# Feed-forward stages: transposes and low-rank product issued one schedule step earlier

## The chip, the cores and the metric

The kernel runs on one core of a Trainium2 chip. The metric is the device time of one execution in microseconds. TensorE (PE), VectorE (DVE), ScalarE (ACT), GpSimd (POOL) and SyncE (SP, which issues DMAs) each run their own instruction stream in order, and meet by semaphores.

## The reference

The input `x` is 8 x 1024 tokens of 256 float32 values. Four layers follow, each added to its own input:

```python
x = x + attn_a(layernorm(x))     # recurrent mixer
x = x + ffn(layernorm(x))
x = x + attn_b(layernorm(x))     # softmax attention, 16 heads
x = x + ffn(layernorm(x))        # the same weights

def ffn(x, fast_b, w_fc, w_proj, u, v, gate):
    h = bitlinear(x, w_fc) + gate * (x @ v.T @ fast_b.T @ u.T)   # 256 -> 1024, and rank 16
    r = maximum(h, 0)
    return bitlinear(r * r, w_proj)                              # 1024 -> 256
```

`bitlinear` multiplies by weights that are rounded to -1, 0 or 1, with a scale per output.

## The kernel before

Each of the four layers is a stage of the kernel, one after the other. The change is in `feed_forward`, which runs twice (names with `ffn_` in the profile; the rest, `a_` and `b_`, is not touched).

A feed-forward stage works on 16 chunks of 512 tokens. The work on a chunk has three parts:

- **normalize**: VectorE finds mean and variance (lines 1217, 1221), GpSimd makes the reciprocal root (1294, 1296), VectorE writes the normalized tokens `xn` in four tiles (1233). TensorE transposes them in two groups of four (1043). ScalarE copies a group to `x_hi`, rounded to the matmul's input format (1120), and VectorE writes the rest, `x_lo` (1240). TensorE makes the low-rank product from both in four matmuls (1053), ScalarE and VectorE turn it into `low` (1128, 1247). The moments of the next chunk are taken at the end of the part.
- **up**: eight times, five matmuls of 512 columns, the fifth with `low` (1065, 1066, 1069). ScalarE applies relu (1137) and square (1141), VectorE splits the square into `r_hi` (1261) and `r_lo` (1263).
- **down**: for each of four token tiles, 16 matmuls of 256 columns (1082, 1083). VectorE scales the result (1274) and GpSimd adds it to `x` (1319).

The parts of three chunks run interleaved: `down(c)`, `up(c + 1)` and `normalize(c + 2)` form one turn. Each part is a Python generator with eight steps. `side_by_side` takes one step of each part in rotation, down first, then up, then normalize, and it does so on every engine for itself:

```python
while running:
    part = min(running, key=lambda r: (r[2] + 0.5) / r[0])
    if next(part[1], running) is running:
        running.remove(part)
    part[2] += 1
```

So the place of an instruction in its engine's queue is set by the step in which its generator issues it. A bare `yield`, or `steps(n)`, which is n of them, is an empty step: it moves what follows behind one more piece of down and of up. A piece of down on TensorE is half a token tile (10 matmuls, then 6), a piece of up is one tile of the hidden layer. There are 18 turns in a stage: the first has normalize alone, the second up and normalize, then come 14 full ones, one without normalize, and one with down alone. Two banks of PSUM hold the transposes and the low-rank product by turns.

Of the kernel before, what the change touches and what calls it, by code (L numbers as in the profile page):

```python
# [906 lines left out]
def feed_forward(nc, banks, x_in, x_out, d, tag, prepared):  # L907
    with nc.cleanup_on_exit(), ExitStack() as ctx:
# [64 lines left out]
        def steps(n):  # L973
            for _ in range(n):
                yield

        def schedule(down, up, normalize):
            for c in range(-2, CHUNKS):
                side_by_side(*([(DOWN, down(c), 1)] if c >= 0 else []),
                             *([(UP, up(c + 1), 1)] if 0 <= c + 1 < CHUNKS else []),  # L980
                             *([(NORMALIZE, normalize(c + 2), 1)] if c + 2 < CHUNKS else []))

        def ternary_turns():

            fc_part = [(m, m, 0, KT) for m in range(HT)]
            return fc_part, [(FC_TURNS + m * (HT // CT) + n, m, n * CT, CT) for m in range(KT) for n in range(HT // CT)]

        def tensor(pe):
            def prepare_weights():
                if not first_use:  # L990
                    pe.wait_ge(kept_moved, 16 * len(kept))
                    return

                def turn_ternary(turns, first_row):
                    for turn, m, at, count in turns:
                        b, s = banks[:, turn % 5, :], tern[(first_row + m) % 2]
                        pe.wait_ge(tern_made, first_row + m + 1)
                        if turn >= 5:
                            pe.wait_ge(tern_t_made, turn - 4)
                        for i in range(count):  # L1000
                            last = pe.transpose(b[:, i * P:(i + 1) * P], s[:, (at + i) * P:(at + i + 1) * P], ident[:, :])
                        last.then_inc(tern_turned, 1)

                fc_part, proj_part = ternary_turns()
                pe.wait_ge(x_lo_made, KT)
                turn_ternary(fc_part, 0)
                pe.wait_ge(weights_in, 16 * WEIGHTS)
                pe.wait_ge(u_steps, 5)
                for m in range(HT):
                    if m >= 2:  # L1010
                        pe.wait_ge(u_t_made, m - 1)
                    pe.transpose(banks[0:ROWS, 5 + m % 2, 0:P], u3[:, m, :], ident[:, :]).then_inc(u_turned, 1)
                for kt in range(KT):
                    if kt:
                        pe.wait_ge(low_copied, 1)
                    pe.matmul(banks[:, 7, 0:RANK], v[:, kt * P:(kt + 1) * P], fast_b[:, :],
                              start=True, stop=True).then_inc(low_product, 1)
                turn_ternary(proj_part, HT)
                for kt in range(KT):
                    pe.wait_ge(diagonal_made, kt + 1)  # L1020
                    if kt:
                        pe.wait_ge(row_made, 1)
                    pe.matmul(banks[:, 7, 0:P], ones[:, :], diagonal[:, kt, :], start=True, stop=True).then_inc(row_ready, 1)
                pe.wait_ge(tern_t_made, FC_TURNS + PROJ_TURNS)
                pe.wait_ge(row_made, KT)
                pe.wait_ge(low_split, 2)
                pe.wait_ge(u_t_made, HT)

            def normalize(c):
                x_hi, x_lo = x_hi_bufs[c % 2], x_lo_bufs[c % 2]  # L1030
                yield from steps(3)
                for kt in range(KT):
                    b = normal[(3 * c + kt) % 2]

                    chunk, part = divmod(3 * c + kt - 2, 3)
                    if chunk >= 0 and part == 2:
                        pe.wait_ge(low_made, chunk + 1)
                    elif chunk >= 0:
                        pe.wait_ge(x_lo_made, 2 * chunk + part + 1)
                    for i in range(CT):  # L1040
                        if kt == 0:
                            pe.wait_ge(xn_made, CT * c + i + 1)
                        last = pe.transpose(b[:, i * P:(i + 1) * P], xn[i][:, kt * P:(kt + 1) * P], ident[:, :])  # L1043
                    last.then_inc(xn_turned, 1)
                    yield
                if c == 0:
                    prepare_weights()
                yield
                b = normal[(3 * c + 2) % 2]
                pe.wait_ge(x_lo_made, 2 * c + 2)  # L1050
                passes = [(kt, w, s) for kt in range(KT) for w, s in ((low_by_hi, x_hi), (low_by_lo, x_lo))]
                for n, (kt, w, s) in enumerate(passes):
                    last = pe.matmul(b[0:ROWS, :], w[:, kt, :], s[:, kt, :], start=n == 0, stop=n == len(passes) - 1)  # L1053
                last.then_inc(low_ready, 1)
                yield from steps(2)

            def up(c):
                x_hi, x_lo, low = x_hi_bufs[c % 2], x_lo_bufs[c % 2], low_bufs[c % 2]
                for m in range(HT):
                    use, cols = HT * c + m, slice(m * P, (m + 1) * P)  # L1060
                    b = high[use % 3]
                    if use >= 3:
                        pe.wait_ge(relu_made, use - 2)
                    for kt in range(KT):
                        pe.matmul(b, fc_t[:, kt, cols], x_hi[:, kt, :], start=kt == 0, stop=False)  # L1065
                        pe.matmul(b, fc_t[:, kt, cols], x_lo[:, kt, :], start=False, stop=False)  # L1066
                    if m == 0:
                        pe.wait_ge(low_made, c + 1)
                    pe.matmul(b, u3_t[:, cols], low[:, :], start=False, stop=True).then_inc(h_ready, 1)  # L1069
                    yield  # L1070

            def down(c):
                par = c % 2
                for i in range(CT):
                    use = CT * c + i
                    b = back[use % 3]
                    if use >= 3:
                        pe.wait_ge(y_scaled, use - 2)
                    for m in range(HT):
                        if i == 0:  # L1080
                            pe.wait_ge(r_lo_made, HT * c + m + 1)
                        pe.matmul(b[:, 0:DIM], r_hi[par][:, m, i * P:(i + 1) * P], proj_t[:, m, :], start=m == 0, stop=False)  # L1082
                        last = pe.matmul(b[:, 0:DIM], r_lo[par][:, m, i * P:(i + 1) * P], proj_t[:, m, :],  # L1083
                                         start=False, stop=m == HT - 1)
                        if m == HT // 2:
                            yield
                    last.then_inc(y_ready, 1)
                    yield

            pe.wait_ge(ident_in, 16)  # L1090
            schedule(down, up, normalize)

        def scalar(act):
# [18 lines left out]

            def normalize(c):
                x_hi, low = x_hi_bufs[c % 2], low_bufs[c % 2]
                yield from steps(3)
                for kt in range(KT):
                    act.wait_ge(xn_turned, 2 * c + kt + 1)
                    if c >= 2:
                        act.wait_ge(h_ready, HT * (c - 1))
                    act.activation(x_hi[:, kt, :], normal[(3 * c + kt) % 2], ACT.Copy).then_inc(x_hi_made, 1)  # L1120
                    yield
                if c == 0:
                    prepare_weights()
                yield
                act.wait_ge(low_ready, c + 1)
                if c >= 2:
                    act.wait_ge(h_ready, HT * (c - 1))
                act.activation(low[:, :], normal[(3 * c + 2) % 2][0:ROWS, :], ACT.Copy).then_inc(low_hi_made, 1)
                yield from steps(2)

            def up(c):
                for m in range(HT):
# [11 lines left out]
            def down(c):  # L1144
                for _ in range(DOWN):
                    yield

            schedule(down, up, normalize)

        def vector(dve):  # L1150
# [73 lines left out]
            def normalize(c):  # L1224
# [7 lines left out]
                for i in range(CT):  # L1232
                    dve.tensor_scalar(xn[i][:, :], x[:, i, :], mean_var[:, i, 0:1], norm_rstd[:, i:i + 1],
                                      ALU.subtract, ALU.mult).then_inc(xn_made, 1)
                yield from steps(2)
                for kt in range(KT):
                    dve.wait_ge(x_hi_made, 2 * c + kt + 1)
                    if c >= 2:
# [4 lines left out]
                if c == 0:  # L1243
# [2 lines left out]
                dve.wait_ge(low_hi_made, c + 1)  # L1246
                dve.tensor_tensor(low[SUB:2 * SUB, :], normal[(3 * c + 2) % 2][SUB:2 * SUB, :],
                                  low[SUB:2 * SUB, :].bitcast(F32), ALU.subtract).then_inc(low_made, 1)
                yield
                if c + 1 < CHUNKS:  # L1250
                    take_moments(c + 1)
                yield
# [904 lines left out]
```

## Time and profile before

| | us |
|---|---|
| median of 3 runs | 3332.47 |
| lowest, highest | 3331.1, 3334.16 |
| profiled execution | 3332.47 |
| its span in the profile | 3330.7 |

The two feed-forward stages take about 375 and 335 us of the span. In the profile an engine is busy while it works on an instruction; matmul ends are modelled, so the start of the next matmul is the better mark. Idle time stands with the event that ended it. A share of busy time says little by itself here; what counts is which wait on TensorE ends last.

### The profile page before, as it was taken

What the parts mean: (1) busy time and instruction counts of PE and PEld (TensorE: products, weight loads), DVE (VectorE), ACT (ScalarE), POOL (GpSimd) and SP (SyncE); (2) the same over time, 40 slices, a digit from 0 to 9 for tenths busy, and PEclk for the clock granted to TensorE, in tenths of its full rate; (3) what the DMA queues carried; (4) which work ended last, traced back from release to release, by engine and by line L of the source; (5) the groups of instructions that cost most, each with busy time, mean ns of one, the idle gap of its engine ahead of it and who ended that gap; (6) DMA issues with size and microseconds to landing.
All of it is one profiled execution on the core that took longest, in us unless ns stands there. A gap on an engine that the chain in (4) does not pass through costs nothing. (4 is left out here: it accounts for less than half of the span.)

```text
span 3330.7 us, 78935 instructions
## 1 busy us (share of the span) xinstructions
PE 3141.0 (94%) x31780; PEld 1962.2 (59%) x31780; DVE 2521.4 (76%) x4844; ACT 1984.0 (60%) x2967; POOL 784.5 (24%) x920
## 2 busy tenths in 40 slices
PE   7999999995999589999999999999999999987999
PEld 3666666663888445555555555555555555546888
DVE  6877777755888368878878788788787887827887
ACT  2545555533666217676767676667676767775665
POOL 3444455432223201011021020110210201011222
PEclk8999999986999759999999999999999999998999
DMA  1000000003111512122222131222221312103111
GB/s 53 15 21 21 27 27 27 21 16 103 51 51 52 108 29 46 25 46 50 46 50 46 25 70 25 46 50 46 50 45 25 70 26 45 37 4 102 51 58 39
DMA packets 110301, 145.50 MB, mean 44 GB/s; under 512 B 21745, under 2 KB 94209, under 8 KB 109153
## 3 DMA queue, kind: packets, MB, share of 16 engines
q1 hardware_dynamic: 108728, 136.78, 17.6%
q8 instruction: 252, 4.13, 0.5%
q0 software_dynamic: 768, 2.77, 0.4%
q10 hardware_dynamic: 440, 0.90, 0.2%
q14 instruction: 113, 0.92, 0.1%
HBM read 53.79 MB, written 38.24 MB: 28 GB/s over the span
## 5 line engine op out<-in xcount | busy, mean ns | idle before, releaser
L1883 DVE TENSOR_REDUCE b_half_max<-banks 128x1 f32<-128x512 f32 x2048 | 1305.0, 685 | 300.9 <-PE banks L1556 184.4
L1807 ACT ACTIVATE b_p_t<-banks 128x1024 f32<-128x1024 f32 x1024 | 1039.6, 1026 | 372.7 <-PE banks L1556 231.6
L1632 PE MATMUL banks<-b_k_stack,b_q_stack 62*128 62x512 f32 x2048 | 836.1, 481 | 35.3 <-issue 19.4
L1694 PE MATMUL banks<-b_q_stack,b_k_stack 64*128 64x512 f32 x2048 | 832.5, 469 | 8.5 <-ACT b_p_t L1807 7.7
L1648 PE MATMUL banks<-b_p_t,b_v 128*17 128x256 f32 x8192 | 628.4, 385 | 0.2 <-ACT b_p_t L1807 0.2
L1694 PEld LDWEIGHTS banks<-b_q_stack,b_k_stack 64*128 64x128 f32 x2048 | 344.5, 185 | 372.8 <-issue 323.2
L1632 PEld LDWEIGHTS banks<-b_k_stack,b_q_stack 62*128 62x128 f32 x2048 | 342.0, 188 | 85.2 <-DVE b_half_max L1883 34.0
L1556 PE MATMUL banks<-b_unit,b_tables 64*128 64x64 bf16 x4096 | 373.3, 197 | 0.0
L1137 ACT ACTIVATE ffn_relu<-banks,ffn_scale_fc 128x512 f32<-128x512 f32 x256 | 176.1, 688 | 206.0 <-PE banks L1069 206.0
L1082 PE MATMUL banks<-ffn_proj_t,ffn_r_hi 128*128 128x256 f32 x1024 | 262.2, 289 | 2.7 <-DVE ffn_r_lo L1263 2.5
L1556 PEld LDWEIGHTS banks<-b_unit,b_tables 64*128 64x128 bf16 x4096 | 186.3, 96 | 120.9 <-issue 72.2
L1083 PE MATMUL banks<-ffn_proj_t,ffn_r_lo 128*128 128x256 f32 x1024 | 253.8, 280 | 0.0
L1648 PEld LDWEIGHTS banks<-b_p_t,b_v 128*17 128x17 f32 x8192 | 142.4, 95 | 168.6 <-ACT b_p_t L1807 59.2
L1972 POOL TENSOR_TENSOR b_qk_lo<-b_qk,b_qk_hi 128x512 fp32r<-128x512 f32 x64 | 81.8, 1279 | 607.7 <-ACT b_qk L1749 461.5
L1082 PEld LDWEIGHTS banks<-ffn_proj_t,ffn_r_hi 128*128 128x128 f32 x1024 | 193.5, 189 | 18.0 <-DVE ffn_r_lo L1263 8.6
L1065 PE MATMUL banks<-ffn_x_hi,ffn_fc_t 128*128 128x512 f32 x512 | 203.3, 397 | 0.0
L1066 PE MATMUL banks<-ffn_x_lo,ffn_fc_t 128*128 128x512 f32 x512 | 202.9, 396 | 0.0
L1083 PEld LDWEIGHTS banks<-ffn_proj_t,ffn_r_lo 128*128 128x128 f32 x1024 | 193.3, 189 | 8.2
L1263 DVE TENSOR_TENSOR ffn_r_lo<-ffn_square,ffn_r_hi 128x512 fp32r<-128x512 f32 x256 | 188.9, 738 | 8.8
L1319 POOL TENSOR_TENSOR ffn_x<-ffn_x,ffn_scaled_out 128x256 f32<-128x256 f32 x128 | 112.9, 882 | 339.8 <-DVE ffn_scaled_out L1274 339.8
L1261 DVE CAST ffn_r_hi<-ffn_square 128x512 fp32r<-128x512 f32 x256 | 127.3, 497 | 74.8 <-ACT ffn_square L1141 73.2
L1141 ACT ACTIVATE ffn_square<-ffn_relu 128x512 f32<-128x512 f32 x256 | 161.9, 632 | 8.1
(246 smaller groups left out, 4941.1 us busy)
## 6 DMA issues: line engine op xcount, KB each, us to landing
ffn_x<-x SPq DMA_DIRECT2D x32, 512.0 KB, 3.9
b_q_stack<-b_qk_hi SPq DMA_DIRECT2D x252, 64.0 KB
b_k_stack<-b_qk_hi SPq DMA_DIRECT2D x252, 64.0 KB
a_x<-hidden_states SPq DMA_DIRECT2D x16, 512.0 KB, 4.2
x<-a_x SPq DMA_DIRECT2D x16, 512.0 KB, 2.9
x<-ffn_x SPq DMA_DIRECT2D x16, 512.0 KB, 2.8
b_x<-x SPq DMA_DIRECT2D x8, 1024.0 KB, 5.7
x<-b_x SPq DMA_DIRECT2D x8, 1024.0 KB, 4.4
```

Of the source, the lines that this page charges most:

```text
L1065: pe.matmul(b, fc_t[:, kt, cols], x_hi[:, kt, :], start=kt == 0, stop=False)
L1066: pe.matmul(b, fc_t[:, kt, cols], x_lo[:, kt, :], start=False, stop=False)
L1082: pe.matmul(b[:, 0:DIM], r_hi[par][:, m, i * P:(i + 1) * P], proj_t[:, m, :], start=m == 0, stop=False)
L1083: last = pe.matmul(b[:, 0:DIM], r_lo[par][:, m, i * P:(i + 1) * P], proj_t[:, m, :], start=False, stop=m == HT - 1)
L1137: act.activation(relu[use % 2][:, :], high[use % 3], ACT.Relu, scale=scale_fc[:, m:m + 1]).then_inc(relu_made, 1)
L1263: dve.tensor_tensor(r_lo[par][:, m, :], square[use % 2][:, :], r_hi[par][:, m, :].bitcast(F32), ALU.subtract).then_inc(r_lo_made, 1)
L1556: last = pe.matmul(out[:, cols], tables[rows, g % GROUPS * PAIRS + pair, 1 - variant, part, :], unit[rows, :], start=False, stop=part == P ...
L1632: last = pe.matmul(m, q_stack[rows, slot, qb * P:(qb + 1) * P], k_stack[rows, slot, half * BANK:(half + 1) * BANK], start=True, stop=not h ...
L1648: last = pe.matmul(values[i * SLOT:i * SLOT + VW, cols], v[:, kb, hg * GROUP + i, :], p_t[(2 * t + i % 2) % P_BUFS][:, i // 2, cols], star ...
L1694: last = pe.matmul(out, k_stack[stack, slot, kb * P:(kb + 1) * P], q_stack[stack, slot, half * BANK:(half + 1) * BANK], start=True, stop=n ...
L1807: act.activation(p_t[use % P_BUFS][:, :, :], scores[use % 2], ACT.Exp, scale=slopes()[pair][0]).then_inc(p_made, 1)
L1883: dve.tensor_reduce(half_max[:, (pair + rg * PAIRS) * QB + qb, half:half + 1], misc.at["max", g, turn], axis=AX.X, op=ALU.max, negate=True ...
```

## The change

Three parts of `normalize` change, one for each of TensorE, ScalarE and VectorE. On all three the empty steps ahead of the first transposes, or of what uses them, are one fewer, and those at the end of the part one more. On VectorE the tiles `xn` stay in the second step and the moments in the eighth. GpSimd's `normalize` is not touched, nor are down, up and SyncE.

```diff
@@ tensor, normalize(c)
-                yield from steps(3)
+                yield from steps(2)
                 for kt in range(KT):
                     b = normal[(3 * c + kt) % 2]
...
                 last.then_inc(low_ready, 1)
-                yield from steps(2)
+                yield from steps(3)
@@ scalar, normalize(c)
-                yield from steps(3)
+                yield from steps(2)
                 for kt in range(KT):
                     act.wait_ge(xn_turned, 2 * c + kt + 1)
...
                 act.activation(low[:, :], normal[(3 * c + 2) % 2][0:ROWS, :], ACT.Copy).then_inc(low_hi_made, 1)
-                yield from steps(2)
+                yield from steps(3)
@@ vector, normalize(c)
                     dve.tensor_scalar(xn[i][:, :], x[:, i, :], mean_var[:, i, 0:1], norm_rstd[:, i:i + 1],
                                       ALU.subtract, ALU.mult).then_inc(xn_made, 1)
-                yield from steps(2)
+                yield
                 for kt in range(KT):
                     dve.wait_ge(x_hi_made, 2 * c + kt + 1)
...
                                   low[SUB:2 * SUB, :].bitcast(F32), ALU.subtract).then_inc(low_made, 1)
-                yield
+                yield from steps(2)
                 if c + 1 < CHUNKS:
                     take_moments(c + 1)
```

The first group of transposes goes from the fourth step to the third, the second from the fifth to the fourth, the low-rank product from the seventh to the sixth, and what ScalarE and VectorE make of each goes with it.

## Rows read from the trace of the kernel before

**Rows 1.** The page, part 1: busy us, share, instructions.
```profile
PE 3141.0 (94%) x31780; PEld 1962.2 (59%) x31780; DVE 2521.4 (76%) x4844; ACT 1984.0 (60%) x2967; POOL 784.5 (24%) x920
```
**Rows 2.** Busy us by stretch, one turn each (PE PEld DVE ACT POOL, clock, DMA).
```profile
879.00:898.00 19.00, 19.00 (x118) 16.61 (x117) 16.48 (x36) 12.03 (x19) 5.34 (x6) 1.00 0.17 56
3182.50:3201.49 18.99, 18.98 (x118) 16.51 (x116) 16.47 (x36) 12.02 (x19) 5.36 (x6) 1.00 0.18 56
```
**Rows 3.** The chain that ended last, second stage: start, us, what.
```profile
3042.13 0.47 PE banks L1043 x4
...
3288.95 0.47 PE banks L1043 x4
3291.77 0.44 PE banks L1043 x4
...
3296.43 0.92 PE banks L1053 x4
```
**Rows 4.** Waits over the whole span: us in total, times, longest.
```profile
PE banks L1043 <- DVE ffn_xn L1233: 32.8, 4, 18.1
PEld banks L1082 <- DVE ffn_r_lo L1263: 8.6, 30, 1.5
```
**Rows 5.** Timeline of one turn, TensorE: start, us, what.
```profile
3184.91 0.40 PE L1069 MATMUL banks<-ffn_low,ffn_u_t 80*128 80x512 f32 x1
...
3187.84 0.28 PE L1083 MATMUL banks<-ffn_proj_t,ffn_r_lo 128*128 128x256 f32 x1
3188.14 0.39 PE L1082 MATMUL banks<-ffn_proj_t,ffn_r_hi 128*128 128x256 f32 x1
...
3189.41 0.39 PE L1069 MATMUL banks<-ffn_low,ffn_u_t 80*128 80x512 f32 x1
...
3191.97 0.29 PE L1082 MATMUL banks<-ffn_proj_t,ffn_r_hi 128*128 128x256 f32 x1
...
3193.86 0.64 PE L1043 MATMUL banks<-ffn_ident,ffn_xn 128*128 128x128 f32 x4
3194.24 0.37 PE L1082 MATMUL banks<-ffn_proj_t,ffn_r_hi 128*128 128x256 f32 x1
```
**Rows 6.** Timeline of the same turn, VectorE (idle time and releaser in brackets).
```profile
3184.39 0.69 DVE L1263 TENSOR_TENSOR ffn_r_lo<-ffn_square,ffn_r_hi 128x512 fp32r<-128x512 f32 x1
...
3185.82 0.42 DVE L1274 TENSOR_TENSOR ffn_scaled_out<-banks,ffn_scale_row 128x256 f32<-128x256 f32 x1
3186.73 0.62 DVE L1261 CAST ffn_r_hi<-ffn_square 128x512 fp32r<-128x512 f32 x1 [0.48 <-ACT ffn_square L1141]
...
3191.23 0.43 DVE L1261 CAST ffn_r_hi<-ffn_square 128x512 fp32r<-128x512 f32 x1
...
3192.30 1.81 DVE L1233 TENSOR_SCALAR ffn_xn<-ffn_x,ffn_mean_var,ffn_norm_rstd 128x256 f32<-128x256 f32 x4
...
3200.58 0.87 DVE L1261 CAST ffn_r_hi<-ffn_square 128x512 fp32r<-128x512 f32 x1 [0.24 <-ACT ffn_square L1141]
```
**Rows 7.** Timeline of the same turn, GpSimd.
```profile
3186.33 0.74 POOL L1319 TENSOR_TENSOR ffn_x<-ffn_x,ffn_scaled_out 128x256 f32<-128x256 f32 x1 [4.16 <-DVE ffn_scaled_out L1274]
...
3200.42 0.74 POOL L1319 TENSOR_TENSOR ffn_x<-ffn_x,ffn_scaled_out 128x256 f32<-128x256 f32 x1 [3.96 <-DVE ffn_scaled_out L1274]
```
**Rows 8.** Timeline of the second stage's second turn, TensorE.
```profile
3024.34 0.39 PE L1066 MATMUL banks<-ffn_x_lo,ffn_fc_t 128*128 128x512 f32 x1
3024.57 0.40 PE L1069 MATMUL banks<-ffn_low,ffn_u_t 80*128 80x512 f32 x1
3025.68 1.21 PE L1043 MATMUL banks<-ffn_ident,ffn_xn 128*128 128x128 f32 x4 [0.71 <-DVE ffn_xn L1233]
...
3031.30 0.46 PE L1053 MATMUL banks<-ffn_x_hi,ffn_low_by_hi 128*80 128x512 f32 x1 [0.45 <-DVE ffn_x_lo L1240]
```
**Rows 9.** TensorE alone by stretch: busy us (instructions), clock, DMA share, GB/s.
```profile
2978.00:2984.00 6.00, 3.57 (x35) 1.00 0.00 0
...
2996.00:3002.00 6.00, 0.00 (x0) 0.50 0.52 175
```

## The prediction

> **What bounds the kernel now.** I read the page first: TensorE is busy for 94% of the span [rows 1]. The change touches only the two feed-forward stages, so their stretches come next. One turn of the schedule has the same busy times in both: TensorE has work in all 19 us at a granted clock of 1.00, VectorE in 16.5, ScalarE in 12.0 [rows 2]. The chain that ended last shows how regular that is. The first transposes of a turn stand at 3042.13 us, those 13 turns later at 3288.95, so a turn lasts 18.99 us [rows 3]. A turn costs what TensorE's queue takes, waits included, and the reader must see which waits are in it. The list of waits gives two. The transposes waited for `xn` four times in the whole run, too few for the 28 full turns. The down product's weight load waited for `r_lo` 30 times, 8.6 us together [rows 4].
>
> **How near the edge that is.** The timelines of one turn, engine by engine, say when each thing is ready. I write Dk, Uk, Nk for the k-th piece of down, up and normalize, T0 and T1 for the two groups of transposes, L for the low-rank products. TensorE's order is D1 U1 N1 D2 U2 N2 and so on. Before, T0 stands in N4, T1 in N5, L in N7, and VectorE writes `xn` in N2.
> - U2's closing matmul starts at 3189.41 [rows 5]. Its result goes through ScalarE to VectorE, whose r_hi starts at 3191.23; r_lo and then the four `xn` follow, 3192.30 to 3194.11 [rows 6].
> - TensorE does D3 and U3 until 3191.97, D4 and U4 until 3193.86, and then T0; D5 begins at 3194.24 [rows 5]. The fourth transpose needs the fourth `xn`, which ended at 3194.11, and D5 begins 0.13 us after that. In the chain T0 takes 0.47 us and T1, whose inputs have long been there, 0.44 [rows 3]. So T0 arrives within some hundredths of the moment from which it would have to wait. There is no slack to spend.
>
> **The change part by part.** No instruction is added or removed: three counts of empty steps change on TensorE, ScalarE and VectorE. `xn` stays in VectorE's N2 and the moments in its N8; T0, T1, L and the conversions behind them go one step forward. GpSimd and SyncE keep their order, and no DMA moves.
>
> *T0 from N4 to N3.* TensorE now reaches T0 at 3191.97 in the picture of that turn, but the fourth `xn` still ends at 3194.11, because what leads to it (U2, ScalarE, r_hi, r_lo, four `xn`) is not moved. TensorE resumes at 3194.24, the same time as before, but with D4 and U4 still to do. Their length is 3191.97 to 3193.86, 1.89 us, and nothing later gives it back, as all that follows is TensorE's own work. Behind the waiting transposes the queue holds D4, U4 and the rest of the turn; ScalarE and VectorE wait for those in turn, and have time to spare. Cost: 1.89 us a turn.
>
> *T1 and L.* T1 follows U4; its inputs are there and its bank is free. In the chain L stands 4.66 us behind T1 (3291.77 to 3296.43), two pieces of down and two of up apart [rows 3], and it will again. Counted from D4's start, L is reached at 1.89 and 4.66, 6.55 us. It needs the second half of x_lo. U4's closing matmul starts at about 1.65, r_hi comes 1.82 us behind a closing matmul (3186.73 after 3184.91), the pair r_hi and r_lo takes 1.15 and x_lo about 0.7 as r_lo does: 5.3 us. So it is covered, by 1.2 us, and beyond that L would wait for the difference. U1 of the next turn, which uses the low result, has it a step sooner than before. Cost: nothing.
>
> *L out of the gap between U7 and U8.* L took 0.92 us [rows 3] between U7 and D8. With it gone, all that hangs on U7 comes 0.92 us later as seen from U8. VectorE's r_lo of U7 ends at 3186.00 in place of 3185.08; the low result, which followed it, is away, so the scaled output starts at 3186.03 [rows 6]. GpSimd's addition starts 0.51 us behind it (3186.33 after 3185.82) and takes 0.74: 3186.54 to 3187.28 [rows 6, 7]. r_hi of U8 starts at 3186.73, inside it. Where they overlap, r_hi ends 0.28 or 0.29 us after the addition does: 3187.35 after 3187.07, and 3201.45 after 3201.16, where it took 0.87 us and not some 0.43 [rows 6, 7]. So r_hi ends at 3187.56. Before it ended at 3187.35: 0.21 us later.
> The Trainium skill (SBUF — State Buffer, section "SBUF: two separate sides") says that VectorE in its fast modes and GpSimd share a pair of ports, and that whoever starts first locks it for the whole instruction. Those rows agree with it. By it the 0.21 us stands as long as GpSimd starts first, which it does here by 0.19 us, and turns into a gain if r_hi comes first.
>
> *The wait for r_lo in D2.* The last pair of D2 needs r_lo of U8. It starts at 3188.14, 0.30 us after the matmul at 3187.84 [rows 5]. 512 columns take 0.23 us [rows 8], so these 256 would take 0.12, and 0.18 us is wait. It stands ahead of U2 in the queue, so the 0.21 us adds to the turn; the `xn` are late by no more than that. 1.89 and 0.21 are 2.10 us a turn. If r_hi of U8 is free of the addition, it takes 0.19 less and the wait goes: 1.89 less 0.18, 1.71 us.
>
> *The second turn of a stage*, the first with up, has no down part. T0 waited there too: U4's closing matmul starts at 3024.57, T0's four run from 3025.68 and wait for the `xn` [rows 8]. Now U4 (five matmuls, 1.17 us) comes after T0. L waited for x_lo at its end (3031.30, 0.45 us idle before it) [rows 8]. It starts at about the same time in its new place, with U7 still to do. Cost: one U, some 1.1 us, in each stage. The last two turns have no normalize and stay as they are. The very first turn holds normalize alone, and its order does not change.
>
> **The sum.** 28 turns of 2.10 us are 58.8, two such second turns 2.2, together 61.0 us. The profiled execution took 3332.47 us, its span 3330.7, and the median of the runs is also 3332.47: 3393.5 us. The bounds: 1.71 us a turn gives 50.1 and 3382.6 us. For the upper one I take one more meeting of VectorE and GpSimd on the chain in each turn, at the 0.43 us that the full one costs r_hi: 2.53 us a turn, 73.0 and 3405.5 us.
>
> **Rivals.**
> 1. *The collision goes away*, as r_hi of U8 begins ahead of the addition. The stall at T0 stays. For it: only 0.19 us separates the two starts. Against: both hang on the same TensorE order by fixed distances. 3382.6 us.
> 2. *The move is hidden*, so not slower. VectorE has 2.5 us without work in a turn [rows 2], and its four `xn` would come 1.9 us sooner if that slack lay ahead of them. This decides from an `xn` end of 3192.2 in the picture of that turn. With the r_lo wait gone as well (28 times 0.18) it gives 3327.4, without it 3332.5 us. Against: U2's own result reaches r_hi at 3191.23 whatever VectorE does before it, and with the pair and four `xn` behind it the end cannot come much before 3194.
> 3. *The clock falls in the pause.* TensorE would stand for some 2 us in each turn. With no work at all from 2996 to 3002 us the granted clock is 0.50, half of 2.4 GHz; with 3.57 us of work in the 6 us from 2978 it stays at 1.00 [rows 9]. If 6 us of each turn ran at half rate, 3 us more would go in each: 28 times 3.0 is 84, 3477 us.
> The Trainium skill (TensorE: Matmul & The Clock Gate, Part 1) says that the gate closes behind idleness and opens with sustained work. By it this rival is real only if such a pause counts as idle; the row at 2978 speaks against it.
>
> **Chances.** The forecast 0.80, the first rival 0.09, the second 0.06, the third 0.05. About 0.2% (6.7 us) is what can be told from no change here. The second rival lies within it, but for 0.01 in which it goes beyond, to faster. So faster 0.01, same 0.05, slower 0.94. The range goes from just below the first rival to the upper bound, 3380 to 3406 us. It leaves out rivals two and three and a little of the forecast's own error.
>
> **What the profile of the changed kernel would show.** A turn of 21.1 us in both stages in place of 18.99. Waits at the transposes for `xn` in all 30 turns, about 1.9 us each, on TensorE's matmul or its weight load. A wait at the down product for r_lo of 0.4 us, with r_hi of U8 at about 0.83 us. No wait of L for x_lo in the full turns. The clock at 1.00 through the turns. A turn of 20.7 us with r_hi of U8 at 0.43 would show the first rival, one of 19.0 the second, matmuls at half rate behind the pause the third. The forecast is wrong if the first `xn` starts earlier than 2.9 us after U2's closing matmul.

## The result and the profile after

The changed kernel takes 3392.99 us (median of 4, 3391.84 to 3396.83), the kernel before 3333.31 us on the same occasions: a ratio of 1.0168, 95% interval 1.0145 to 1.0192. It is 1.7% slower, and the forecast was 3393.5 us. The profiled execution has a span of 3394.8 us, 64.1 us more than before.

The chain that ended last in the second stage, for [rows 3] (start, us, what). T0 of one turn and of the next:

```profile
3201.92 0.83 DVE ffn_xn L1233
...
3202.89 1.21 PE banks L1043 x4
...
3210.63 0.92 PE banks L1053 x4
...
3223.93 1.21 PE banks L1043 x4
...
3350.27 1.21 PE banks L1043 x4
```

T0 comes every 21.05 us (from 3202.89 to 3350.27 are 7 turns) in place of 18.99. In the chain it is 1.21 us long and was 0.47, and the first `xn` is now a link ahead of it.

The stretches of one turn and of 13 turns, for [rows 2] (length, busy us of PE, PEld, DVE, ACT, POOL, then the granted clock, DMA share and GB/s):

```profile
3202.89:3223.93 21.04, 19.71 (x116) 16.52 (x117) 16.21 (x36) 12.12 (x20) 5.17 (x6) 1.00 0.15 46
```

```profile
3076.59:3350.27 273.68, 256.21 (x1509) 214.79 (x1509) 211.00 (x456) 157.67 (x248) 67.28 (x78) 1.00 0.14 47
```

The work is the same, TensorE has 1.3 us of each turn without any, and the clock stays at its upper level through all 13 turns. The list of waits, for [rows 4] (us in total, times, longest):

```profile
PE banks L1043 <- DVE ffn_xn L1233: 66.0, 32, 18.5
PEld banks L1082 <- DVE ffn_r_lo L1263: 14.9, 30, 1.5
PEld banks L1043 <- DVE ffn_xn L1233: 11.0, 60, 0.2
PE banks L1082 <- DVE ffn_r_lo L1263: 8.8, 30, 1.3
```

The wait for `xn` is now in the 28 full turns too. It has grown by 33.2 us; 2.3 of them lie in the two second turns, and the rest is 1.10 us in each full turn. That is less than the loss. The timeline of TensorE shows why, for [rows 5]:

```profile
3220.09 0.39 PE L1069 MATMUL banks<-ffn_low,ffn_u_t 80*128 80x512 f32 x1
...
3222.43 0.40 PE L1069 MATMUL banks<-ffn_low,ffn_u_t 80*128 80x512 f32 x1
3223.93 1.21 PE L1043 MATMUL banks<-ffn_ident,ffn_xn 128*128 128x128 f32 x4 [1.10 <-DVE ffn_xn L1233]
3224.90 0.37 PE L1082 MATMUL banks<-ffn_proj_t,ffn_r_hi 128*128 128x256 f32 x1
...
3231.52 0.39 PE L1053 MATMUL banks<-ffn_x_hi,ffn_low_by_hi 128*80 128x512 f32 x1
...
3239.36 0.28 PE L1083 MATMUL banks<-ffn_proj_t,ffn_r_lo 128*128 128x256 f32 x1
3239.88 0.38 PE L1082 MATMUL banks<-ffn_proj_t,ffn_r_hi 128*128 128x256 f32 x1 [0.24 <-DVE ffn_r_lo L1263]
```

U3's closing matmul starts at 3222.43 and would be followed 0.23 us later. D4 begins at 3224.90, so T0 takes 2.24 us of the queue, and took 0.38. The loss is 1.86 us. The profile writes only 1.10 of it down as idle, the rest lies mostly between the four transposes, each of which waits for its own `xn`: they are stretched over 1.21 us. VectorE and GpSimd in the same turns, for [rows 6, 7]:

```profile
3222.97 1.78 DVE L1233 TENSOR_SCALAR ffn_xn<-ffn_x,ffn_mean_var,ffn_norm_rstd 128x256 f32<-128x256 f32 x4
...
3229.52 0.68 DVE L1240 TENSOR_TENSOR ffn_x_lo<-banks,ffn_x_hi 128x512 fp32r<-128x512 f32 x1
...
3237.57 0.42 DVE L1274 TENSOR_TENSOR ffn_scaled_out<-banks,ffn_scale_row 128x256 f32<-128x256 f32 x1
3238.25 0.85 DVE L1261 CAST ffn_r_hi<-ffn_square 128x512 fp32r<-128x512 f32 x1 [0.26 <-ACT ffn_square L1141]
```

```profile
3222.40 1.24 POOL L1319 TENSOR_TENSOR ffn_x<-ffn_x,ffn_scaled_out 128x256 f32<-128x256 f32 x1
...
3238.07 0.74 POOL L1319 TENSOR_TENSOR ffn_x<-ffn_x,ffn_scaled_out 128x256 f32<-128x256 f32 x1 [4.55 <-DVE ffn_scaled_out L1274]
```

The fourth `xn` ends at 3224.75, D4 begins 0.15 us later. GpSimd's addition of 3222.40 lies over the first `xn`, which takes 0.83 us in the chain. The addition of 3238.07 starts 0.18 us ahead of r_hi of U8, which takes 0.85 us, and the last pair of D2 starts 0.52 us after the matmul ahead of it, 0.40 more than without a wait. x_lo's second half ends at 3230.20, and L starts at 3231.52, 1.3 us behind it, without a wait.

The second turn of the second stage, for [rows 8]: TensorE was idle for 1.88 us ahead of T0 in place of 0.71, and for 0.47 ahead of L in place of 0.45.

```profile
3059.66 1.21 PE L1043 MATMUL banks<-ffn_ident,ffn_xn 128*128 128x128 f32 x4 [1.88 <-DVE ffn_xn L1233]
...
3065.27 0.46 PE L1053 MATMUL banks<-ffn_x_hi,ffn_low_by_hi 128*80 128x512 f32 x1 [0.47 <-DVE ffn_x_lo L1240]
```

In the second turn of the first stage T0 waits for 1.96 us in place of 0.79, and there the clock falls. The stretches of 3 us, with all engines, then the clock:

```profile
821.00:824.00 3.00, 1.40 (x5) 0.97 (x6) 2.93 (x8) 1.16 (x3) 0.78 (x1) 0.87 1.01 381
824.00:827.00 3.00, 3.00 (x11) 2.36 (x11) 1.18 (x2) 1.43 (x3) 0.00 (x0) 0.56 0.66 209
```

```profile
822.60 1.35 PE L1043 MATMUL banks<-ffn_ident,ffn_xn 128*128 128x128 f32 x4 [1.96 <-DVE ffn_xn L1233]
...
824.61 0.63 PE L1065 MATMUL banks<-ffn_x_hi,ffn_fc_t 128*128 128x512 f32 x1
825.03 0.63 PE L1066 MATMUL banks<-ffn_x_lo,ffn_fc_t 128*128 128x512 f32 x1
```

Matmuls of 512 columns start 0.42 us apart there, and 0.23 us apart in the same place before.

### The profile page after: what moved, and what is told of

Same layout as the page of the kernel before. It is cut to its first block and busy times, and to the rows that moved or that the text cites. A ratio compares the mean times of both kernels' runs of the same rounds, so it can differ in the third digit from the quotient of the medians.

```text
span 3394.8 us, 78935 instructions
## 1 busy us (share of the span) xinstructions
PE 3167.3 (93%) x31780; PEld 1968.3 (58%) x31780; DVE 2514.9 (74%) x4844; ACT 1986.9 (59%) x2967; POOL 779.7 (23%) x920
## 5 line engine op out<-in xcount | busy, mean ns | idle before, releaser
L1082 PEld LDWEIGHTS banks<-ffn_proj_t,ffn_r_hi 128*128 128x128 f32 x1024 | 194.4, 190 | 24.4 <-DVE ffn_r_lo L1263 14.9
L1263 DVE TENSOR_TENSOR ffn_r_lo<-ffn_square,ffn_r_hi 128x512 fp32r<-128x512 f32 x256 | 177.3, 692 | 8.8
```

## The experiments

Two things were to be tested: that the stall at T0 is the distance from U2's result to the fourth `xn` and nothing about the place itself, and that the smaller part is GpSimd's addition meeting r_hi. All kernels compute the whole reference. Turn lengths are distances from one L to the next in full turns. Each ratio is to executions of the kernel before on the same occasions, and not to the 3334.27 in the first row: their median is 3333.31 us for the changed kernel, 3333.78 for the two parts alone, one step more and early moments without the hold, 3334.27 for the rest. One long execution moves a ratio more than it moves a median (the transposes alone have one of 3399.86 us), so the turns tell kernels apart better than the ratios do.

| kernel | turn, us | median, us | ratio to before, 95% interval |
|---|---|---|---|
| before | 18.98 | 3334.27 (23 runs) | |
| changed | 21.05 | 3392.99 (4) | 1.0168, 1.0145 to 1.0192 |
| transposes alone | 20.83 | 3387.29 (4) | 1.0168, 1.0144 to 1.0192 |
| L alone | 20.34 | 3374.21 (4) | 1.0124, 1.0109 to 1.0140 |
| transposes one step more | 24.99 | 3510.29 (4) | 1.0539, 1.0519 to 1.0559 |
| `xn` in N1 | 20.13 | 3369.11 (4) | 1.0101, 1.0088 to 1.0114 |
| `xn` in N1, early moments | 19.18 | 3340.69 (10) | 1.0016, 0.9999 to 1.0033 |
| changed, addition held | 20.65 | 3386.05 (4) | 1.0153, 1.0139 to 1.0166 |
| before, addition held | 18.80 | 3327.36 (12) | 0.9991, 0.9977 to 1.0006 |
| early moments, addition held | 18.78 | 3327.20 (12) | 0.9978, 0.9966 to 0.9990 |

**Transposes alone.** Against the changed kernel, on TensorE (and the same on ScalarE and VectorE):

```diff
                 if c == 0:
                     prepare_weights()
-                yield
+                yield from steps(2)
                 b = normal[(3 * c + 2) % 2]
...
                 last.then_inc(low_ready, 1)
-                yield from steps(3)
+                yield from steps(2)
```

> Only the transposes and x_hi, x_lo go a step forward; the low-rank product L stays in N7. Theory (the fourth xn decides, and L's leaving the gap between U7 and U8 makes the 0.2 us): a turn of 20.88 us (18.99 and 1.89), r_hi of U8 at 0.62 us as before, the wait for r_lo at 0.18 us; 28 times 1.89 and some 1.4 in the second turns, 3387 us. Rival (the later r_lo comes with the transposes, not with L): a turn of 21.06 us and r_hi of U8 at 0.85, 3392 us.

The turn is 20.83 us. VectorE's r_hi of U8:

```profile
3191.65 0.62 DVE L1261 CAST ffn_r_hi<-ffn_square 128x512 fp32r<-128x512 f32 x1 [0.48 <-ACT ffn_square L1141]
```

0.62 us, as before. The list of waits has the load's row for r_lo back at `8.6, 30, 1.5`. The move of the transposes costs 1.85 us a turn and leaves r_hi alone; the other 0.22 us come with L.

**L alone.** Against the kernel before, the `yield` ahead of L goes behind it, on the three engines.

```diff
                 if c == 0:
                     prepare_weights()
-                yield
                 b = normal[(3 * c + 2) % 2]
...
                 last.then_inc(low_ready, 1)
-                yield from steps(2)
+                yield from steps(3)
```

> Only the low-rank product L goes a step forward, to N6; transposes stay in N4 and N5. Theory: in the turn of the trace of before L would be reached at 3198.99, while the second half of x_lo ends at 3200.01, so L waits 1.1 us, and the addition meets r_hi of U8 for 0.21 us more: a turn of 20.3 us, 3371 us. Rival (L costs only the meeting, 0.21 us a turn): 3338 us. No wait at the transposes in either.

```profile
3192.10 0.46 PE L1052 MATMUL banks<-ffn_x_hi,ffn_low_by_hi 128*80 128x512 f32 x1 [0.93 <-DVE ffn_x_lo L1238]
...
3200.51 0.38 PE L1081 MATMUL banks<-ffn_proj_t,ffn_r_hi 128*128 128x256 f32 x1 [0.23 <-DVE ffn_r_lo L1260]
```

On TensorE's timeline L waits for x_lo and D2's last pair for r_lo, as expected; the turn is 20.34 us, 1.36 more than before. So the parts do not add (1.85 and 1.36 alone, 2.07 together): with the transposes a step earlier x_lo comes earlier too, and L's own wait of 1.1 us is covered.

**Transposes one step more.** On TensorE and ScalarE the first group goes to N2, the second to N3; L stays in N6.

```diff
-                yield from steps(2)
+                yield from steps(1)
                 for kt in range(KT):
...
                 if c == 0:
                     prepare_weights()
-                yield
+                yield from steps(2)
```

> Transposes another step forward (first group in N2, second in N3), L in N6. Theory: TensorE reaches the first group 2.33 us (D3 and U3) earlier still, the fourth xn ends at the same distance from U2, so a turn of 23.4 us and some 3459 us, with the granted clock at 1.00. Rival (the clock falls in a pause of 4.2 us a turn): matmuls of 512 columns spaced 0.43 us behind the pause in the turns, 80 us more. Rival (the price is not the distance to xn): no more than the changed kernel, 3393 us.

The theory's time was missed by 51 us. The turn is 24.99 and not 23.4 us. TensorE by stretches of 4 us (length, busy, instructions, granted clock, DMA share, GB/s), and its timeline:

```profile
3200.00:3204.00 4.00, 3.77 (x24) 1.00 0.33 112
3204.00:3208.00 4.00, 0.55 (x4) 0.89 0.44 145
3208.00:3212.00 4.00, 4.00 (x16) 0.50 0.01 5
3212.00:3216.00 4.00, 4.00 (x20) 0.76 0.01 4
3216.00:3220.00 4.00, 4.00 (x27) 1.00 0.00 0
```

```profile
3207.93 1.35 PE L1043 MATMUL banks<-ffn_ident,ffn_xn 128*128 128x128 f32 x4 [3.45 <-DVE ffn_xn L1233]
```

From its list of waits:

```profile
PE banks L1043 <- DVE ffn_xn L1233: 133.3, 32, 18.1
```

The idle time at T0 grew by 67.3 us against the changed kernel; in a full turn it is 3.45 us in place of 1.10, 2.35 more, where 2.33 was expected. The turn grew by 3.94 us. The other 1.6 us go with the clock: by the end of the 3.45 us it has fallen to 0.50, 1.2 GHz, and matmuls run at half rate until it rises. The idle time is the same in every full turn while the turns take 24.4 to 25.8 us, so what varies is not the wait. The rival on the clock, which the full turns of the changed kernel did not show with 1.10 us idle, is real at this length: the kernel takes 51 us more than expected, where the rival had 80.

**`xn` in N1**, in the changed kernel. The wait for `norm_scale` and the four `xn` go ahead of VectorE's first `yield`, and that `yield` behind them.

```diff
                     take_moments(c)
-                yield
                 dve.wait_ge(norm_scale, c + 1)
...
                                       ALU.subtract, ALU.mult).then_inc(xn_made, 1)
-                yield
+                yield from steps(2)
```

> The changed kernel with xn issued in N1 and not N2; moments and reciprocal root stay in the eighth step. Theory (the price of the transposes' place is the time at which the fourth xn ends): xn no longer waits for U2's result but for the reciprocal root, which ends 0.9 us before xn could end now less its own 1.4 us; the fourth xn ends 0.9 us sooner, the turn is 20.2 us, 3368 us. Rival (what is ahead of xn does not matter, the transposes cost by their place): 3393 us.

VectorE's timeline:

```profile
3202.01 1.38 DVE L1232 TENSOR_SCALAR ffn_xn<-ffn_x,ffn_mean_var,ffn_norm_rstd 128x256 f32<-128x256 f32 x4 [0.93 <-POOL ffn_norm_rstd L1295]
```

`xn` now waits for the reciprocal root. The turn is 20.13 us. The transposes stand where they stood, and the loss went from 2.07 to 1.15 us by what ends `xn`. About 0.4 of the gain has a cause that the expectation did not name: the four `xn` take 1.38 us in place of 1.78, as no addition lies over the first of them now.

**`xn` in N1 and early moments.** The same, and the moments of the next chunk in VectorE's fifth step, the reciprocal root in GpSimd's sixth.

```diff
                 if c == 0:
                     prepare_weights()
+                if c + 1 < CHUNKS:
+                    take_moments(c + 1)
                 yield
...
-                yield from steps(2)
-                if c + 1 < CHUNKS:
-                    take_moments(c + 1)
-                yield
+                yield from steps(3)
@@ gpsimd, normalize(c)
-                yield from steps(3)
+                yield
                 if c + 1 < CHUNKS:
                     take_rstd(c + 1)
-                yield
+                yield from steps(3)
```

> The change as it is, with xn moved from VectorE's N2 to N1, and the moments and the reciprocal root that it needs moved from the eighth step to the fifth and sixth. Theory: the fourth xn is there before TensorE reaches the transposes in N3, so that wait goes and only the r_lo wait of 0.39 us stays: a turn of 19.2 us, 3334 to 3338 us. Rival (the earlier place of the transposes costs by something else, a bank or the order itself): the turn stays near 21 us, 3390 us.

From the list of waits, and VectorE's and GpSimd's timelines:

```profile
PE banks L1043 <- DVE ffn_xn L1232: 32.0, 4, 18.1
PEld banks L1082 <- DVE ffn_r_lo L1261: 16.6, 32, 1.5
```

```profile
3208.58 0.43 DVE L1259 CAST ffn_r_hi<-ffn_square 128x512 fp32r<-128x512 f32 x1
3209.05 1.11 DVE L1261 TENSOR_TENSOR ffn_r_lo<-ffn_square,ffn_r_hi 128x512 fp32r<-128x512 f32 x1
```

```profile
3208.66 0.95 POOL L1317 TENSOR_TENSOR ffn_x<-ffn_x,ffn_scaled_out 128x256 f32<-128x256 f32 x1 [1.23 <-DVE ffn_scaled_out L1272]
```

With the transposes in N3 the wait for `xn` is back at four times in the run. The turn is 19.18 us; the median is a little above what was expected. What is left is the r_lo wait, and in a form that the prediction did not have: r_hi starts first and takes 0.43 us, but the addition, which waits for it, then holds up r_lo, 1.11 us in place of 0.69. The trace of the kernel before has the same pattern, in the very turn that the prediction read:

```profile
3195.44 0.43 DVE L1261 CAST ffn_r_hi<-ffn_square 128x512 fp32r<-128x512 f32 x1
3195.90 1.11 DVE L1263 TENSOR_TENSOR ffn_r_lo<-ffn_square,ffn_r_hi 128x512 fp32r<-128x512 f32 x1
```

```profile
3195.58 0.88 POOL L1319 TENSOR_TENSOR ffn_x<-ffn_x,ffn_scaled_out 128x256 f32<-128x256 f32 x1 [2.60 <-DVE ffn_scaled_out L1274]
```

**The held addition**, in three kernels. GpSimd's fourth addition of a chunk waits until r_lo of U8 is made:

```diff
                     pool.wait_ge(y_scaled, use + 1)
+                    if i == CT - 1 and c + 1 < CHUNKS:
+                        pool.wait_ge(r_lo_made, HT * (c + 2))
```

> The changed kernel, with GpSimd's fourth addition of a chunk held until r_lo of U8 is made, so that it can't meet r_hi or r_lo of U8. Theory (the meeting costs 0.4 us on the chain r_hi, r_lo, down product, and the wait for r_lo is nothing but that and 0.0 us): r_hi of U8 0.43 us, no wait for r_lo in D2, a turn of 20.66 us in place of 21.06, 3382 us. Rival (r_hi takes 0.85 us for another reason, or the held addition meets something else on the chain): the turn stays at 21.06, 3393 us. The wait at the transposes stays in both.

> The kernel before, with the same hold on the fourth addition. Theory: r_hi of U8 0.43 in place of 0.62 us, the wait of 0.18 us for r_lo goes, a turn of 18.81 us, 5 us less than before in all. Rival (the held addition delays the moments, the reciprocal root or xn, and the transposes, which have no slack, then wait): a turn of 19.0 us or more, no gain or a loss.

> The kernel with xn in N1 and early moments, with the same hold. In the trace without it the addition starts 0.08 us after r_hi of U8 and r_lo takes 1.11 us in place of 0.69; the turn is 19.17 us. Theory: both go back to 0.43 and 0.69, no wait for r_lo, a turn of 18.8 us and 10 us less than without the hold, which is below the kernel before. Rival: the turn stays at 19.17, as the r_lo wait there has another cause.

The changed kernel with the hold, VectorE and its list of waits:

```profile
3208.97 0.43 DVE L1261 CAST ffn_r_hi<-ffn_square 128x512 fp32r<-128x512 f32 x1 [0.26 <-ACT ffn_square L1141]
3209.43 0.69 DVE L1263 TENSOR_TENSOR ffn_r_lo<-ffn_square,ffn_r_hi 128x512 fp32r<-128x512 f32 x1
```

```profile
PEld banks L1082 <- DVE ffn_r_lo L1263: 2.4, 2, 1.2
```

The r_lo wait is gone from the full turns of all three, and each turn is within 0.03 us of what was expected: 20.65, 18.80 and 18.78 us. For the changed kernel and the one before, the intervals of the times are too wide to show it; there the turns do. The third kernel has the lowest ratio, 0.22% below the one before, and its interval ends 0.10% below. The kernel before with the hold has nearly the same median and turn, but an interval that reaches 1; which of the two is better is not settled.

## Why the prediction was right

- *No slack at T0, and 1.89 us a turn by its move*: 1.86 in the turn shown, 1.85 with the transposes alone. The first `xn` starts 2.88 us after U2's closing matmul (3222.97 after 3220.09). By the letter that is the prediction's sign of being wrong, earlier than 2.9 us, but the kernel before has 2.89 (3192.30 after 3189.41), so the bound was set by rounding and nothing moved. That the end of `xn` sets it, and not the place, is shown by moving `xn` with T0 where it is: the loss shrinks (20.13) and vanishes (19.18, and 18.78 with the hold).
- *What the path to `xn` held and the prediction did not name*: in the kernel before, too, an addition (3191.72, 1.26 us) lies over the first `xn`, and the four take 1.81 us where they take 1.38 without it. Without this meeting T0 would have had some 0.4 us of slack; that is an estimate, as no run holds that addition alone.
- *The meeting with r_hi, 0.21 us*: 0.22 us from the turns with and without L's move. r_hi took 0.85 us where 0.83 was forecast, the r_lo wait 0.40 where 0.4 was. Holding the addition takes all of it away, 0.40 us a turn.
- *T1 and L at no cost*: covered by 1.3 us, 1.2 forecast. L alone cost 1.1 us for x_lo. The term is nothing because x_lo's own place is earlier as well, as the prediction had counted.
- *The sum*: 28 turns of 2.07 us are 58.0 us, where 58.8 was forecast; the difference of the medians is 59.7 us. The profiled execution has 64.1 us more. Of these, 3.0 lie ahead of the first stage's first L (815.19 for 812.16), where the change alters no order; in the ten traces this L stands between 809.2 and 815.8 us, so they are not a cost of the change. From that L to the end it is 61.1 us more, where 61.0 was forecast.
- *The second turns* were put at a U each, 1.1 us, and at nothing else. T0's idle time does grow by 1.17 us in both. But in the first stage the clock falls behind it, and T1 starts 3.29 us after T0 in place of 2.21, 1.1 us that the prediction did not have. In the second stage the clock stays at 1.00 there, and rises some 1.4 us sooner after the first L than before, which gives a part back. That the total still agrees within 0.1 us is luck, and so is the half microsecond between forecast and median: four executions of the changed kernel lie between 3391.84 and 3396.83 us.
- *The second rival, hidden*, fell: all 28 turns wait. *The first*, no collision, did not come about, and its mechanism was wrong as put. In the kernel with early moments r_hi is ahead of the addition and there is no gain; the addition then meets r_lo, at the same price. *The third*, the clock, did not come about in the full turns with 1.10 us idle. It did in one second turn with 1.96, and it does in every full turn with 3.45.
- *What the profile would show* was off in one point: not 1.9 us each in the list of waits but 1.10 on the first matmul, since the rest of the pause is spread between the four transposes.

## What to carry to other kernels

In a schedule interleaved by hand, moving an instruction a step ahead is worth something only if its inputs have slack. Compare, in the timeline, the end of the last input with the moment at which the engine now reaches the instruction. Here they met within some hundredths of a microsecond, and the move forward cost the whole length of what it overtook (1.85 of 1.89 us), because the bounding engine then waited with that work behind it. A part moved out of a gap also shifts everything chained to the two sides of the gap; here that brought an addition of GpSimd over more of a VectorE operation, 0.22 us. And two moves that cost alone may cover for each other, so the costs of parts need not add.

Look also at what makes the last input late. Here a part of it was again an addition of GpSimd over the operation, 0.4 us that could be read from the trace before the change.

## What the runs showed of the hardware

- A GpSimd addition of 128x256 costs VectorE up to about 0.4 us, whichever starts first. If the addition starts 0.18 us ahead, r_hi takes 0.85 us and not 0.43; at 0.40 us ahead it takes 0.62. If r_hi starts 0.08 us ahead, the addition takes longer (0.95 us and not 0.74) and the next VectorE operation pays (1.11 us and not 0.69). This agrees with the rule of the Trainium skill (SBUF — State Buffer, "SBUF: two separate sides") that the pair of ports is locked for a whole instruction. But the prediction had drawn a gain from it for the case in which VectorE comes first; with its operations back to back there is none.
- TensorE's granted clock stayed at 1.00 through 13 turns with 1.10 us idle and four spread transposes in each, and fell to 0.50 in every full turn with 3.45 us idle.
- In the second turns idle times near 1.9 us went both ways: the clock fell behind 1.96 us in the changed kernel's first stage and behind 1.87 us with the transposes alone (second stage), and stayed at 1.00 behind 1.88 and 1.96 us in the second stage of the changed kernel without and with the hold.
